# Four chained graph layers: in the relation stage every second gathered tile is turned by a transposing DMA instead of by TensorE

## The chip, the cores and the metric

The kernel runs on one core of one Trainium2 chip. The metric is device time in microseconds: the median of several executions, from which one execution was also recorded by the hardware profiler.

## The reference, cut to what matters

A feature matrix `x` of 1250 nodes by 768 goes through four graph layers (attention, GCN, attention with 12 heads, relational GCN), each followed by a residual sum and a layer norm. 20000 edges with one of 34 types each are given. The change lies in the fourth layer:

```python
seg  = edge_type * n + dst
agg  = segment_sum(x[src], seg, 34 * n)
mean = agg.reshape(34, n, -1) / maximum(cnt, 1).reshape(34, n, 1)
h1   = einsum('rni,rio->no', mean, W_rel) + x @ W_root + b_rgcn   # W_rel: 34 x 768 x 768
```

## The kernel before, in words

The fourth layer computes a message for each edge, not for each mean. Edges are sorted by relation and cut into RT = 190 tiles of P = 128 edges that hold one relation each, some 5.6 tiles to a relation. For a tile, 128 rows of `x3` are gathered, multiplied by that relation's 768 x 768 matrix, scaled by 1/count, and stored in `msg_d`; a later stage sums the messages by destination.

Numbers are float32, and the product is made in three parts, each operand being split into a rounded high part and the rest: high by high, high by low, low by high. A tile's product is 36 matmuls of 128 x 128 by 384: two halves of the output, three parts, KC = 6 blocks of 128 features. TensorE wants features on the partitions, so gathered rows (edges on partitions) are turned first, six 128 x 128 blocks to a tile.

The relation stage runs on all five sequencers, each in its own program order, tied by counting semaphores:

- **POOL** (`pool_rel`): gathers tile k+4 (L1885) into one of four row buffers `rows7` once tile k is turned, then subtracts for the low part of tile k (`low`, L1890).
- **PE** (`pe_rel`): turns tile k+2 into PSUM banks 0 to 3 (`turn`, L1912), then multiplies tile k into banks 4 to 7 (`messages`, L1924), two tiles deep.
- **ACT** (`act_rel`): `store` scales the product of tile k out of PSUM (L1961) and issues its DMA to `msg_d` (L1964); then `take` copies the turned tile k+3 twice out of PSUM, in full (L1953) and rounded (L1955), and raises `s_take7` (L1956), for which POOL's `low` and PE's next turn wait.
- **SP** (`sp_rel`): loads the next relation's matrix (L1853) as soon as the plain copy is split.
- **DVE** (`dve_rel`): splits that matrix into high and low (L1860, L1861) into the half of `wsplit` that the last but one relation has left.

Ahead of it the root stage handles the ten node tiles of `x3`: DVE sums and normalizes a tile (`rows`, with ACT's square root, L414, in the middle), POOL stores it to `x3_d` (L1821), PE turns it (L324) and multiplies it by `W_root` (L306), ACT copies the turned tile (L341), DVE adds the bias (L1792). The first gather waits for all ten stores.

Of the kernel before, what the change touches and what calls it, by code (L numbers as in the profile page):

```python
# [19 lines left out]
P = 128  # L20
# [3 lines left out]
D = 768  # L24
# [51 lines left out]
def build(nc, a, out):  # L76
    ctx = ExitStack()
    with ctx:
# [15 lines left out]
        x3_d = dram("x3_d", (NP, D))  # L94
        msg_d = dram("msg_d", (RT * P, D))
# [1678 lines left out]
        s_ready6, s_bias6 = sem("x3_ready"), sem("root_bias_in")  # L1774
        brow6 = work[:, 3 * KC * D:3 * KC * D + D]

        def dve_root(v, step):


            def rows(j):  # L1780
                z = z6[:, j, :]
                v.wait_ge(s_parts6[j % 2], 32 * (j // 2 + 1))
                step(v.tensor_tensor(z, z, parts6[0][:, j % 2, :], ALU.add))
                step(v.scalar_tensor_tensor(z, z, 0.0, parts6[1][:, j % 2, :], ALU.max, ALU.add))
                norm6.vector(v, step, z, j)
                v.sem_inc(s_ready6, 1)

            def product(j):
                if j == 0:
                    v.wait_ge(s_bias6, 16)  # L1790
                v.wait_ge(W_ROOT.product, W_ROOT.b["product"] + j + 3)
                v.tensor_tensor(halves(hbuf[:, j * D:(j + 1) * D]), W_ROOT.psum(j % 2), halves(brow6), ALU.add).then_inc(W_ROOT.emptied, 1)  # L1792
                if j == 7:
                    v.wait_ge(s_wrel, 16)
                    for u in range(2):
                        v.wait_ge(s_st6[u], 16 * (NT // 2))
                if j >= 7:
                    for c in (2 * (j - 7), 2 * (j - 7) + 1):
                        split7(v, step, 0, c)

            step.wait()
            for j in range(NT):
                rows(j)
                if j >= 2:
                    product(j - 2)
            for j in range(NT - 2, NT):
                product(j)

        def act_root(act):
            for j in range(2):  # L1810
                norm6.scalar(act, j)
            for j in range(NT):
                W_ROOT.take(act, j // 2, j % 2)
                if j + 2 < NT:
                    norm6.scalar(act, j + 2)

        def pool_root(g, step):
# [4 lines left out]
            for u in range(2):  # L1822
                g.wait_ge(s_st6[u], 16 * (NT // 2))

# [3 lines left out]
        rows7 = c7(GW * D).rearrange("p (u r n) -> p u r n", u=GW, r=1)  # L1828
        xt7 = c7(2 * D).rearrange("p (u c n) -> p u c n", u=2, c=KC)
        msg7 = c7(2 * D).rearrange("p (u n) -> p u n", u=2)  # L1830
        rows8 = c7(BT, I32)
# [5 lines left out]
        s_gath = [sem(f"rows_gathered{u}") for u in range(GW)]  # L1837
        s_turn7, s_take7, s_prod7, s_emp7, s_lo7 = (sem(n) for n in ("turned7", "taken7", "product7", "emptied7", "low_parts7"))
        s_split7 = sem("weights_split7")

        def sp_rel(sp):
# [6 lines left out]
            sp.dma_start(w, rel[0]).then_inc(s_wrel, 16)  # L1848
            for j in range(2, NT):
                sp_parts(sp, j)  # L1850
            with sp.Fori(0, R - 1) as i:
# [51 lines left out]
        def pe_rel(pe):  # L1903
# [3 lines left out]
            def turn(u, gathers, k):  # L1907
                pe.wait_ge(s_gath[u % GW], 16 * gathers)
                if not isinstance(k, int) or k >= 2:
                    pe.wait_ge(s_take7, k - 1)  # L1910
                for c in range(KC):
                    last = pe.transpose(ps[:, 2 * (u % 2) + c // 3, (c % 3) * P:(c % 3 + 1) * P], rows7[:, u % GW, 0, c * P:(c + 1) * P], ident[:, :])  # L1912
# [16 lines left out]
            for k in range(2):  # L1929
                turn(k, 1, k)  # L1930
            pe.wait_ge(W_ROOT.emptied, W_ROOT.b["emptied"] + NT + 2)
            whole = (RT - 2) // GW
            with pe.Fori(0, whole) as i:
                for u in range(GW):

                    turn(u + 2, i + 1 + (u + 2) // GW, GW * i + u + 2)
                    messages(GW * i + u, u)
            for k in range(whole * GW, RT):
                if k + 2 < RT:
                    turn(k + 2, (k + 2) // GW + 1, k + 2)  # L1940
                messages(k, k % GW)

        def act_rel(act, step):
# [3 lines left out]
            def take(k, u):  # L1947
                act.wait_ge(s_turn7, k + 1)
# [4 lines left out]
                step.count(act.activation(xt7[:, u % 2].rearrange("p (a b) n -> p a (b n)", a=2),  # L1953
                                          ps[:, 2 * (u % 2):2 * (u % 2) + 2, 0:HALF], ACT.Copy))
                step(act.activation(halves(xhi7[:, u % XW, :]), ps[:, 2 * (u % 2):2 * (u % 2) + 2, 0:HALF], ACT.Copy))  # L1955
                act.sem_inc(s_take7, 1)  # L1956

            def store(k, u, stores):
                act.wait_ge(s_prod7, k + 3)
                act.wait_ge(s_msgst[u % 2], 16 * stores)  # L1960
# [6 lines left out]
            for u in range(2):  # L1967
                act.sem_inc(s_msgst[u], 16)
            for k in range(2):
                take(k, k)  # L1970
            take(2, 2)
            for k in range(2):
                store(k, k, 1)
                take(k + 3, k + 3)
            whole = (RT - 5) // XW
            with step.loop(whole, 3 * XW) as i:
                for u in range(XW):
                    k = XW * i + u + 2
                    store(k, u + 2, 2 * i + 1 + (u + 2) // 2)
                    take(k + 3, u + 5)  # L1980
            for k in range(whole * XW + 2, RT):
                store(k, k, k // 2 + 1)
                if k + 3 < RT:
                    take(k + 3, k + 3)
            for u in range(2):
                act.wait_ge(s_msgst[u], 16 * (RT // 2 + 1))
# [219 lines left out]
```

## Time and profile before

| | |
|---|---|
| median of 3 runs | 3857.95 us (3854.33 to 3860.22) |
| the profiled execution | 3849.39 us, its span 3847.8 us |
| mean granted TensorE clock | 0.972 |
| PE busy | 3577.7 us, 93% of the span |
| ACT, DVE, POOL busy | 1667.7, 1926.0 and 1762.4 us |
| DMA | 468.18 MB, 122 GB/s on average |

The span runs from the first to the last instruction. Busy times are sums over an engine's instructions. The relation stage lies between 2065.8 us (its first turn) and 3386.2 us (its last store) of the span.

### The profile page before, as it was taken

To read this page: it belongs to the slowest core of one execution; us is meant where nothing else is said; L and a number is where in the kernel's file an instruction comes from. 1 tells how busy PE (TensorE), PEld (TensorE's weight loads), DVE (VectorE), ACT (ScalarE), POOL (GpSimd) and SP (SyncE) were. 2 spreads that over 40 slices of the span, in tenths; PEclk is the share of its full clock that TensorE was granted. 3 is DMA by queue.
4 is the path that set the end of the run, shared out by engine and by line. 5 is a ranking of instruction groups with operands and counts; after the bars stand their busy time and mean duration, and the time that the engine had idled before them with its cause. 6 is when DMAs were issued, how large, how long until landed. Compare 5 with 4: busy or idle time off the path is not lost.

```text
span 3847.8 us, 56876 instructions
## 1 busy us (share of the span) xinstructions
PE 3577.7 (93%) x18232; PEld 2940.5 (76%) x18233; DVE 1926.0 (50%) x2740; ACT 1667.7 (43%) x2919; POOL 1762.4 (46%) x1329
## 2 busy tenths in 40 slices
PE   8999779999798996799989999999999999989998
PEld 4654359999798995233347999999999999955598
DVE  8427788887335446999855233322333231023334
ACT  1117878888433212799942333333333333300021
POOL 6888888756100001776003444444444444357600
PEclk9999979999899998899989999999999999999999
DMA  3321123332423113211034555455555553379901
GB/s 109 104 61 23 35 55 86 90 87 63 132 80 121 45 62 103 74 42 42 28 119 153 188 188 186 166 188 187 186 175 173 187 188 114 102 267 305 271 17 69
DMA packets 176799, 468.18 MB, mean 122 GB/s; under 512 B 46100, under 2 KB 62539, under 8 KB 176677
## 3 DMA queue, kind: packets, MB, share of 16 engines
q0 software_dynamic: 59584, 185.70, 16.1%
q1 hardware_dynamic: 83972, 190.43, 15.0%
q10 hardware_dynamic: 33120, 90.52, 6.7%
q8 instruction: 64, 1.05, 0.1%
q14 instruction: 59, 0.48, 0.0%
HBM read 346.22 MB, written 119.79 MB: 121 GB/s over the span
## 4 chain that ended last, share of the span: by engine, by line
PE 41%; ACT 7%; POOL 5%; issue 3%; DVE 2%; DMA 1%; SPq 0%; POOLq 0%; DVEq 0%; ACTq 0%
PE ps L1924 31%; POOL work L2005 5%; ACT work L1304 4%; PE ps L1912 3%; ACT ps L1295 3%; PE ps L1587 3%; PE ps L306 2%; PE ps L298 2%; DVE work L1126 1%; PE ps L1241 1%; DVE work L1154 0%; ACT work L1314 0%; DMA ct<-x_d 0%; DMA work<-msg_d,ct 0%; PE ps L324 0%
## 5 line engine op out<-in xcount | busy, mean ns | idle before, releaser
L1924 PE MATMUL ps<-wsplit,xsplit 128*128 x6840 | 1237.2, 337 | 2.7 <-DVEq L1863 2.7
L1924 PEld LDWEIGHTS ps<-wsplit,xsplit 128*128 128x128 f32 x6840 | 1181.7, 188 | 3.0 <-issue 2.9
L1890 POOL TENSOR_TENSOR xsplit<-ct,xsplit 128x768 fp32r<-128x768 f32 x190 | 369.6, 1945 | 297.4 <-ACTq L1956 297.3
L1860 DVE CAST wsplit<-wplain 128x768 fp32r<-128x768 f32 x204 | 117.2, 574 | 759.8 <-PE ps L1924 743.0
L1304 ACT ACTIVATE work<-ps,work 128x418 f32<-128x418 f32 x720 | 438.4, 632 | 108.5 <-PE ps L1214 102.8
L1961 ACT ACTIVATE ct<-ps,invs 128x768 f32<-128x768 f32 x190 | 171.5, 903 | 710.8 <-PE ps L1924 710.8
L1251 PE MATMUL ps<-hbuf,work 128*128 128x193 f32 x2400 | 455.5, 328 | 15.2 <-DVE work L1168 13.1
L1251 PEld LDWEIGHTS ps<-hbuf,work 128*128 128x128 f32 x2400 | 408.4, 190 | 42.5 <-issue 16.8
L1295 ACT ACTIVATE ps<-work,lr 128x418 f32<-128x418 f32 x720 | 431.6, 634 | 6.1 <-DMA work<-lrow_d 6.1
L1154 DVE SCALAR_TENSOR_TENSOR work<-work,cnt 128x1250 f32<-128x1250 f32 x240 | 349.5, 1456 | 133.9 <-ACT work L1304 131.5
L1885 POOL DMA_INDIRECT ct<-x_d,relrec x190 | 200.9, 1057 | 454.8 <-PE ps L1912 443.2
L1241 PE MATMUL ps<-work,hbuf 128*65 128x512 f32 x720 | 324.6, 533 | 36.6 <-DVE work L1154 34.8
L298 PE MATMUL ps<-wsplit,xsplit 128*128 128x384 f32 x1800 | 337.3, 346 | 12.7 <-DVE xsplit L369 11.5
L298 PEld LDWEIGHTS ps<-wsplit,xsplit 128*128 128x128 f32 x1800 | 322.9, 195 | 14.9 <-issue 12.5
L800 POOL DMA_INDIRECT row_d<-hbuf x160 | 255.7, 1598 | 50.8 <-issue 48.5
L800 POOL DMA_INDIRECT relrec_d<-work x160 | 253.0, 1581 | 48.8 <-issue 48.8
L1214 PE MATMUL ps<-work 128*128 128x418 bf16 x720 | 247.6, 345 | 28.6 <-DMA work<-shift_d 24.3
L1348 POOL DMA_INDIRECT invs<-inv_d,relrec x190 | 220.0, 1158 | 118.1 <-issue 61.4
L2019 PE MATMUL ps<-work 128*128 128x384 f32 x784 | 256.8, 489 | 12.2 <-DMA work<-msg_d,ct 12.1
L1861 DVE TENSOR_TENSOR wsplit<-wplain,wsplit 128x768 fp32r<-128x768 f32 x204 | 246.0, 1206 | 7.1
L800 POOL DMA_INDIRECT dstrec_d<-work x160 | 215.9, 1349 | 66.3 <-issue 48.5
L2019 PEld LDWEIGHTS ps<-work 128*128 128x128 f32 x784 | 148.9, 191 | 119.8 <-issue 14.3
(217 smaller groups left out, 4254.1 us busy)
## 6 DMA issues: line engine op xcount, KB each, us to landing
wplain<-in_L_gnn_W_rel SPq DMA_DIRECT2D x34, 2304.0 KB, 9.5
msg_d<-ct ACTq DMA_DIRECT2D x190, 384.0 KB, 2.6
work<-lrow_d SPq DMA_DIRECT2D x47, 625.0 KB, 3.9
feat_d<-work ACTq DMA_DIRECT2D x30, 386.0 KB, 2.6
hbuf<-feat_d SPq DMA_DIRECT2D x60, 193.0 KB, 2.5
gat_d<-work POOLq DMA_DIRECT2D x12, 960.0 KB, 5.4
xplain<-gat_d SPq DMA_DIRECT2D x30, 384.0 KB, 3.1
wplain<-x_d SPq DMA_DIRECT2D x20, 384.0 KB, 3.1
```

What stands on the lines that cost most here:

```text
L298: last = pe.matmul(ps[:, 4 + 2 * u + h, 0:HALF], x[:, u, c * P:(c + 1) * P], w[:, c * D + h * HALF:c * D + (h + 1) * HALF], start=(q == 0 ...
L800: g.indirect_dma_start(out=(dstrec_d, relrec_d, row_d)[which], out_offset=bass.IndirectOffsetOnAxis((addr[:, 1, t:t + 1], addr[:, 0, t:t + ...
L1154: v.scalar_tensor_tensor(p[:, 0:N], p[:, 0:N], 1.0, cnt3[:, q % NT, 0:N], ALU.min, ALU.mult).then_inc(self.s_p, 1)
L1214: pe.matmul(ps[:, b, 0:c1 - c0], self.ones128, self.crow[h % 2][:, c0:c1], start=False, stop=True, skip_group_check=True).then_inc(self.s_ ...
L1241: last = pe.matmul(ps[0:C + 1, 3 + k, 0:n1 - n0], self.feat(h, s), p[:, n0:n1], start=(s == 0), stop=(s == NT - 1))
L1251: last = pe.matmul(ps[:, self.b0 + b, t * (C + 1):(t + 1) * (C + 1)], p[:, dt * P:(dt + 1) * P], self.feat(h, s), start=(s == 0 and t == 0 ...
L1295: act.activation(ps[:, b, 0:c1 - c0], self.Rb[h % 2][:, c0:c1], ACT.Relu, bias=lr[:, col:col + 1]).then_inc(self.s_relu, 1)
L1304: act.activation(self.p[q % 3][:, c0:c1], ps[:, b, 0:c1 - c0], ACT.Exp, bias=self.l2[:, col:col + 1], scale=1.0 - SLOPE)\
L1861: step(v.tensor_tensor(wlo7[:, at:at + D], w, whi7[:, at:at + D].bitcast(F32), ALU.subtract))
L1890: g.tensor_tensor(xlo7[:, k % XW, :], xt7[:, k % 2].rearrange("p c n -> p (c n)"), xhi7[:, k % XW, :].bitcast(F32), ALU.subtract).then_inc ...
L1924: last = pe.matmul(ps[:, 4 + 2 * (u % 2) + h, 0:HALF], x[:, u, c * P:(c + 1) * P], w[:, bass.ds(base + (c * D + h * HALF), HALF)], start=( ...
L2019: last = pe.matmul(ps[:, 2 * (u % 2) + h, 0:HALF], sel8[:, GT * (u % 2) + w, :], mg8[:, GT * u + w, h * HALF:(h + 1) * HALF], start=(w == ...
```

## The change

The tiles of even number go on as before: they are gathered as float32 rows into `rows7`, now one buffer, and PE turns them. The tiles of odd number are not turned by PE. A transposing DMA moves 2-byte elements, so `x3` is stored a second time with each row's 768 low half-words ahead of its 768 high half-words (`x3p_d`). An odd tile gathers rows of this copy into one of two buffers (`halfs7`), ACT issues one SBUF-to-SBUF transposing DMA of 128 x 1536 half-words into `plane7`, and ACT's `take` puts the half-words together: one copy of 1536 elements with interleaved output in place of the full copy from PSUM, then the rounded copy from SBUF. The buffers fill the room of the four former row buffers.

In the root stage ACT makes each tile's planes ahead of its `take`, SP stores them, the split of the first matrix waits for the planes of all tiles, and the first gather for their stores. `plane6` is the room of `msg7`, and its stores count on the semaphores of the message stores.

```diff
 # act_root, sp_rel, pool_root, dve_root
             for j in range(NT):
+                act.wait_ge(s_ready6, j + 1)
+                if j >= 2:
+                    act.wait_ge(s_msgst[j % 2], 16 * (j // 2))
+                act.activation(plane6[:, j % 2, :].rearrange("p (t n) -> p t n", t=2),
+                               z6[:, j, :].bitcast(U16).rearrange("p (n t) -> p t n", t=2), ACT.Copy).then_inc(s_plane6, 1)
                 W_ROOT.take(act, j // 2, j % 2)
...
+            def planes(j):
+                sp.wait_ge(s_plane6, j + 1)
+                sp.dma_start(x3p_d[j * P:(j + 1) * P, :], plane6[:, j % 2, :]).then_inc(s_msgst[j % 2], 16)
             for j in range(2, NT):
                 sp_parts(sp, j)
+                planes(j - 2)
...
                 g.wait_ge(s_st6[u], 16 * (NT // 2))
+                g.wait_ge(s_msgst[u], PLANES)
...
                     v.wait_ge(s_wrel, 16)
+                    v.wait_ge(s_plane6, NT)
 # pool_rel
             def gather(k):
-                if k >= GW:
-                    g.wait_ge(s_turn7, k - GW + 1)
-                g.indirect_dma_start(out=rows7[:, k % GW, 0, :], out_offset=None, in_=x3_d,
+                if k % 2 == 0 and k >= 2:
+                    g.wait_ge(s_turn7, k // 2)
+                if k % 2 == 1 and k >= 5:
+                    g.wait_ge(s_cross7, 16 * ((k - 4) // 2 + 1))
+                g.indirect_dma_start(out=rows7 if k % 2 == 0 else halfs7[:, k // 2 % 2, :], out_offset=None,
+                                     in_=x3_d if k % 2 == 0 else x3p_d,
...
-            for k in range(GW):
+            for k in (1, 0, 3):
                 gather(k)
             for k in range(RT):
-                if k + GW < RT:
-                    gather(k + GW)
+                ahead = k + (2 if k % 2 == 0 else 4)
+                if ahead < RT:
+                    gather(ahead)
                 low(k)
 # pe_rel
+                for u in range(2, XW + 2):
+                    k = XW * i + u
+                    if u % 2 == 0:
+                        turn(u + 2, i + 1 + (u + 2) // XW, k + 2)
+                    messages(k, u % XW)
 # act_rel
+            def cross(u, gathers, taken=True):
+                act.wait_ge(s_gath[u % GW], 16 * gathers)
+                if taken:
+                    act.sem_inc(s_take7, 1)
+                act.dma_start_transpose(plane7.rearrange("p (c r) -> p c r", r=P), halfs7[:, u // 2 % 2, :]).then_inc(s_cross7, 16)
...
+                if u % 2 == 0:
+                    pair = ps[:, 2 * (u // 2 % 2):2 * (u // 2 % 2) + 2, 0:HALF]
+                    step.count(act.activation(halves(x), pair, ACT.Copy))
+                    step(act.activation(halves(xhi7[:, u % XW, :]), pair, ACT.Copy))
+                else:
+                    step(act.activation(x.bitcast(U16).rearrange("p (n t) -> p t n", t=2), plane7.rearrange("p (t n) -> p t n", t=2), ACT.Copy))
+                    step(act.activation(xhi7[:, u % XW, :], x, ACT.Copy))
+                    act.sem_inc(s_take7, 1)
...
             with step.loop(whole, 3 * XW) as i:
                 for u in range(XW):
                     k = XW * i + u + 2
                     store(k, u + 2, 2 * i + 1 + (u + 2) // 2)
-                    take(k + 3, u + 5)
+                    take(k + 3, u + 5, 2 * i + (u + 5) // 2 + 1)
+                    if u % 2 == 1:
+                        cross(u + 6, i + (u + 6) // XW + 1)
```

Before the loop ACT issues the transfer of tile 1, takes tiles 0, 1 and 2, issues that of tile 3, and goes on in the loop's order.

## Rows read from the trace of the kernel before

**Rows 1.** Page, engines: busy us (share of the span) and instructions.
```profile
PE 3577.7 (93%) x18232; PEld 2940.5 (76%) x18233; DVE 1926.0 (50%) x2740; ACT 1667.7 (43%) x2919; POOL 1762.4 (46%) x1329
```

**Rows 2.** Busy time by stretch: engines' busy us, granted clock, DMA share, GB/s.
```profile
2200.00:2600.00 400.00, 400.00 (x2431) 398.00 (x2430) 124.58 (x140) 139.91 (x174) 174.71 (x116) 1.00 0.53 179
2600.00:3000.00 400.00, 400.00 (x2429) 398.01 (x2428) 120.00 (x136) 139.42 (x174) 175.68 (x116) 1.00 0.54 185
```

**Rows 3.** Waits by pair, 2100 to 3386 us: us in total, times, longest.
```profile
DVE wsplit L1860 <- PE ps L1924: 743.0, 32, 23.6
ACT ct L1961 <- PE ps L1924: 689.2, 186, 5.3
POOL ct L1885 <- PE ps L1912: 423.1, 178, 2.8
```

**Rows 4.** Timeline, ACT's stores of tiles 0, 186, 187, 188 and 189.
```profile
2080.30 0.90 ACT L1961 ACTIVATE ct<-ps,invs 128x768 f32<-128x768 f32 x1 [8.24 <-PE ps L1924]
...
3366.80 0.90 ACT L1961 ACTIVATE ct<-ps,invs 128x768 f32<-128x768 f32 x1 [3.63 <-PE ps L1924]
...
3373.71 0.90 ACT L1961 ACTIVATE ct<-ps,invs 128x768 f32<-128x768 f32 x1 [3.89 <-PE ps L1924]
...
3379.95 0.91 ACT L1961 ACTIVATE ct<-ps,invs 128x768 f32<-128x768 f32 x1 [5.34 <-PE ps L1924]
...
3386.19 0.90 ACT L1961 ACTIVATE ct<-ps,invs 128x768 f32<-128x768 f32 x1 [5.34 <-PE ps L1924]
```

**Rows 5.** Timeline of one tile in mid-stage.
```profile
2605.77 0.82 PE L1912 MATMUL ps<-ident,ct 128*128 128x128 f32 x6
2606.15 0.90 ACT L1961 ACTIVATE ct<-ps,invs 128x768 f32<-128x768 f32 x1 [3.80 <-PE ps L1924]
...
2606.34 6.50 PE L1924 MATMUL ps<-wsplit,xsplit 128*128 x36
2606.86 0.96 POOL L1885 DMA_INDIRECT ct<-x_d,relrec  x1 [2.01 <-PE ps L1912]
2607.30 0.34 ACTq L1964 DMA_DIRECT2D msg_d<-ct  x1
2607.84 0.81 ACT L1953 ACTIVATE ct<-ps 128x768 f32<-128x768 f32 x1 [0.79 <-ACT ct L1961]
2608.55 0.81 ACT L1955 ACTIVATE xsplit<-ps 128x768 fp32r<-128x768 f32 x1
2609.48 1.85 POOL L1890 TENSOR_TENSOR xsplit<-ct,xsplit 128x768 fp32r<-128x768 f32 x1 [1.66 <-ACTq L1956]
```

**Rows 6.** DMA issues by line: count, KB each, median us to landing.
```profile
wplain<-in_L_gnn_W_rel SPq DMA_DIRECT2D x34, 2304.0 KB, 9.5
msg_d<-ct ACTq DMA_DIRECT2D x190, 384.0 KB, 2.6
...
ct<-x_d,relrec POOLq DMA_INDIRECT x190, 4.6
...
shift_d<-work SPq DMA_DIRECT2D x96, 1.9 KB, 1.4
```

**Rows 7.** L1964's own view: its DMA's landing times.
```profile
DMA to landing us min/median/max: 2.3/2.6/7.7
```

**Rows 8.** DMA queue of the scatters, 200 to 400 us: packets, MB, share of 16 engines.
```profile
q0 software_dynamic: 3824, 0.71, 8.2%
```

**Rows 9.** Timeline of the root stage: its start, one tile, its end.
```profile
1986.90 0.20 ACT L414 ACTIVATE small<-small 128x1 f32<-128x1 f32 x1 [13.77 <-DVE small L407]
1987.01 0.79 ACT L341 ACTIVATE ct<-ps 128x768 f32<-128x768 f32 x1
...
1989.46 10.25 PE L306 MATMUL ps<-mask,ct 128*128 128x384 f32 x24
...
2012.60 0.20 ACT L414 ACTIVATE small<-small 128x1 f32<-128x1 f32 x1 [7.50 <-DVE small L407]
2012.71 0.79 ACT L341 ACTIVATE ct<-ps 128x768 f32<-128x768 f32 x1
...
2017.00 7.91 PE L306 MATMUL ps<-mask,ct 128*128 128x384 f32 x24
...
2046.19 0.20 ACT L414 ACTIVATE small<-small 128x1 f32<-128x1 f32 x1 [7.50 <-DVE small L407]
...
2051.01 0.55 DVE L1860 CAST wsplit<-wplain 128x768 fp32r<-128x768 f32 x1
2051.30 1.14 POOL L1885 DMA_INDIRECT ct<-x_d,relrec  x1 [2.81 <-DMA x_d<-work]
...
2066.08 1.47 PE L1912 MATMUL ps<-ident,ct 128*128 128x128 f32 x12
...
2067.17 0.97 POOL L1885 DMA_INDIRECT ct<-x_d,relrec  x1 [10.06 <-PE ps L1912]
...
2072.11 8.15 PE L1924 MATMUL ps<-wsplit,xsplit 128*128 x36 [2.70 <-DVEq L1863]
```

More of the change, by code:

```diff
@@ L1848, in sp_rel @@
             sp.dma_start(w, rel[0]).then_inc(s_wrel, 16)
+            def planes(j):
+                sp.wait_ge(s_plane6, j + 1)
+                sp.dma_start(x3p_d[j * P:(j + 1) * P, :], plane6[:, j % 2, :]).then_inc(s_msgst[j % 2], 16)
             for j in range(2, NT):
                 sp_parts(sp, j)
+                planes(j - 2)
+            for j in range(NT - 2, NT):
+                planes(j)
             with sp.Fori(0, R - 1) as i:
@@ L1908, in turn @@
                 pe.wait_ge(s_gath[u % GW], 16 * gathers)
-                if not isinstance(k, int) or k >= 2:
-                    pe.wait_ge(s_take7, k - 1)
+                if not isinstance(k, int) or k >= 4:
+                    pe.wait_ge(s_take7, k - 3)
                 for c in range(KC):
-                    last = pe.transpose(ps[:, 2 * (u % 2) + c // 3, (c % 3) * P:(c % 3 + 1) * P], rows7[:, u % GW, 0, c * P:(c + 1) * P], ident[:, :])
+                    last = pe.transpose(ps[:, 2 * (u // 2 % 2) + c // 3, (c % 3) * P:(c % 3 + 1) * P], rows7[:, c * P:(c + 1) * P], ident[:, :])
                 last.then_inc(s_turn7, 1)
@@ L1927, in messages @@
                 last.then_inc(s_prod7, 1)
-            for k in range(2):
-                turn(k, 1, k)
+            turn(0, 1, 0)
             pe.wait_ge(W_ROOT.emptied, W_ROOT.b["emptied"] + NT + 2)
-            whole = (RT - 2) // GW
+            turn(2, 1, 2)
+            messages(0, 0)
+            messages(1, 1)
+            whole = (RT - 4) // XW
             with pe.Fori(0, whole) as i:
[L1934 to L1941, printed above, removed]
+                for u in range(2, XW + 2):
[3 more added lines that the diff above has]
+                    messages(k, u % XW)
+            for k in range(whole * XW + 2, RT):
+                if k % 2 == 0 and k + 2 < RT:
+                    turn(k + 2, (k + 2) // XW + 1, k + 2)
+                messages(k, k % XW)
         def act_rel(act, step):
@@ L1966, in act_rel @@
             act.sem_inc(s_emp7, 2)
[L1967 to L1975, printed above, removed]
+            cross(1, 1, taken=False)
+            take(0, 0, 1)
+            act.sem_inc(s_take7, 1)
+            take(1, 1, 1)
+            take(2, 2, 2)
+            cross(3, 1)
+            store(0, 0, 1)
+            take(3, 3, 2)
+            store(1, 1, 1)
+            take(4, 4, 3)
+            cross(5, 2)
+            whole = (RT - 6) // XW
             with step.loop(whole, 3 * XW) as i:
@@ L1983, in act_rel @@
                 if k + 3 < RT:
-                    take(k + 3, k + 3)
+                    take(k + 3, k + 3, (k + 3) // 2 + 1)
+                    if k % 2 == 1:
+                        cross(k + 4, (k + 4) // XW + 1)
             for u in range(2):
-                act.wait_ge(s_msgst[u], 16 * (RT // 2 + 1))
+                act.wait_ge(s_msgst[u], PLANES - 16 + 16 * (RT // 2 + 1))
         UP = 4
```

24 lines of the change are left out of this document (15 added, 9 removed).

## The prediction, made before the changed kernel ran

> **What bounds the kernel now.** I read the page's engine line first: PE is busy for 93% of the span [rows 1]. That is a mean over stages, so I cut the relation stage into stretches: there PE is busy for every one of 400 us, at a granted clock of 1.00 (the 2.4 GHz level), while ACT is busy for 140 us, POOL for 175 and the DMA engines for 0.53 to 0.54 of the time [rows 2]. The waits say the same from the other side: ACT, DVE and POOL all wait for PE, ACT 689 us in 186 waits [rows 3], and PE waits for nobody. So what leaves PE's queue comes off the time, as long as ACT, which gets the work, still ends first.
>
> The price of a turn is seen best in ACT's stores, which follow the products. From tile 0 to tile 187 they are (3373.71 - 2080.30) / 187 = 6.917 us apart, and each of these steps holds one turn. The last two tiles have no turn ahead of them, since all tiles are turned by then: 6.24 us each [rows 4]. A turn thus costs PE 0.677 us, a little more than the 0.57 us between its first transpose and the first product matmul [rows 5].
>
> **What the change takes from PE.** Of the 187 steps, the 94 with an odd tile lose their turn: 94 x 0.677 = 63.6 us. Nothing is added to PE's queue. A pair of tiles goes from 13.83 to 2 x 6.24 + 0.677 = 13.16 us.
>
> **What it gives to ACT.** Before, a tile costs ACT 3.21 us, from the start of its store (2606.15) to the end of the rounded copy (2608.55 + 0.81), the issue of the message's DMA (0.34 us) included; then it idles 3.6 to 3.9 us until the next product ends [rows 4, 5]. In a pair after the change it does, in this order: store and even take, 3.21 us; the wait for the odd tile's gather and the issue of its transposing transfer, c; store of the next tile, 0.90 + 0.79 = 1.69 us; the wait for the transfer's landing, L after its issue began; the odd take. That take is two copies one after the other. By the rows, 1 element costs 0.20 us and 768 cost 0.81 [rows 5, 9], which is 0.8 ns an element, so 1536 elements cost 0.20 + 1.23 = 1.43 us; no row has 2-byte elements interleaved, so I bound it by 0.81 and by twice as much, 2.9, and take 1.43. With the second copy (0.81) and 0.16 of gaps, 2.4 us. ACT's shortest pair is 3.21 + max(L, c + 1.69) + 2.4 us. It stays under PE's 13.16 as long as L is at most 7.55 us and c at most 5.86.
>
> **L and c** are what the trace does not show. From below: 384 KB from the same queue, the message store, land in 2.6 us [rows 6]. From above: a block row of 128 half-words is 256 B, so a tile is 128 x 12 = 1536 pieces. The scatters, the rows with small packets, take 0.082 x 16 x 200 / 3824 = 69 ns a packet [rows 8]; 1536 x 69 / 16 = 6.6 us, and with the landing of a tiny transfer, 1.4 us [rows 6], L = 8.0 us. The gather (the same bytes into SBUF, 4.6 us, rows 6) is the nearest row; the finer pieces put L above it. I take 5.3 us, the middle. Higher still lies a transfer that turns its twelve 128 x 128 blocks one after another: 12 x 1.4 = 16.8 us; that is a rival below. c is bounded by one DMA issue of 0.34 us and twelve of them, 4.1 [rows 5]; both are inside 5.86, so c costs nothing in the steady state. With L = 5.3 ACT's pair is 10.9 us, 2.2 us short of PE's, and hidden.
>
> Two rules of the Trainium skill disagree about L. "DMA: Bandwidth & Descriptors", section "Latency and other measured facts", gives a transposing DMA 261 GB/s in one kernel: by it, as an estimate, 393 KB take 1.5 us and L is near 2.9, well hidden. "VectorE: DVE Perf Modes", section "The three transpose paths", gives the DMA 1309 ns for one 128 x 128 block of 2-byte elements, against 390 for TensorE: twelve times that is 15.7 us, an estimate, and the change would lose heavily. No row of this trace has such a transfer.
>
> **Waits added, and who stands behind them.** Behind the wait for the gather on ACT stand the rise of `s_take7` for the even tile and the next store. That gather is issued once the same buffer's transfer two pairs earlier has landed, some 26 us ahead of its use less L, against 4.6 us of landing: hidden. The even tiles now have one row buffer: POOL gathers the next when PE has turned the last, and the next turn comes 13.16 us later; issue 0.96 and landing 4.6 us leave 7.6 us. POOL's low part of an even tile (1.85 us) is released by ACT some 3.3 us after the tile's turn and is wanted two tiles after it: hidden. Odd `take` plus low part end about 13 us after the release of ACT's pair, and the tile's product starts 20 us after it: 7 us in hand.
>
> **Root stage.** Each tile gains a plane copy, 1.43 us, and a 384 KB store. PE sets the pace there, its 24 matmuls filling 7.91 us of 8.4; ACT idles 7.50 us a tile [rows 9]. In mid-stage the copy moves the end of the turned tile's copy from 2013.5 to 2014.9, and the matmuls that want it begin at 2017.0. At the start it moves 1987.8 to 1989.2, the matmuls beginning at 1989.46; at 2.9 us it would cost 1.2 us once. At the end: from 2046.4 two plane copies and one take (3.65 us) put the last plane at 2050.0, and DVE's split, which now waits for it, starts at 2051.01. SP issues the plane stores between loads that are a tile early. The first gather moves from 2051.3 to between 2052.7 and 2058 (landing as in [rows 7]), and its rows are wanted at 2066. I cost all that at 0.
>
> **Start of the relation stage.** The gather of tile 2 now waits for the turn of tile 0: as the one at 2067.17, it lands 4.6 us later, at 2071.8, and its turn stands ahead of the first product: 2072.45 against 2072.11 [rows 9]. Before its first take ACT issues a transfer; take and low part (3.4 us) after 2066.9 + c hold the product up once c is over 1.8 us, by 2.3 us at c = 4.1. I take 1 us for both.
>
> **Sum** on the profiled execution: 3849.4 - 63.6 + 1 = 3786.8 us. That execution lies 8.6 us under the median of the runs (3857.95), and on the median's footing it is **3795 us**, 1.6% less.
>
> **Rivals.**
> 1. Hidden only in part: the packet price, L = 8.0. ACT's pair is 13.6 us, the gain 0.22 x 95 - 1 = 20 us: 3838. For it: pieces are small and 0.54 of the DMA engines' time is taken; against it: the packets of the scatters go to scattered rows in DRAM. From L of about 8.1 to 8.3 on, no change: 3850 to 3866.
> 2. Slower: ACT becomes the bound. Place: the wait of the odd take for the transfer. Point: L over 8.2 us (7.55 + 0.677). Price: 95 us for each us of L beyond it; L = 10 gives (10 - 7.55) x 95 - 62.6 = +170, **4028 us**. For it: message stores land in 2.6 us at the median but in 7.7 at worst [rows 7]; were the transfer tripled so in one pair of each relation, as the matrix of 2304 KB loads (33 loads of 9.5 us), those pairs would run 8.4 us over, of which the second PSUM buffer covers some 5.3, and 33 x 3.1 = 102 us are lost: 3897. Against it: the bytes, which are those of a message.
> 3. The blocks go one after another, L = 16.8: ACT's pair is 22.4 us, +9.25 x 95 - 62.6 = +816: 4674.
> 4. The change does not do what it says: a turn's 0.677 us is partly a break between products that stays. Then the 0.57 us of the transposes alone come off: 3805, inside the forecast's own range.
>
> **Chances.** Forecast with rival 4, 0.54 (3785 to 3810); rival 1, 0.09, and no change, 0.06; rival 2, 0.23; rival 3, 0.08. The measurement of this kernel tells about 0.2% (7.7 us) from nothing. Faster 0.63, same 0.06, slower 0.31. The range of 8 in 10 goes from 3783 to 4030: it leaves out rival 3, the worst third of rival 2 and a little below. The likeliest case alone: 3785 to 3810.
>
> **What would show it.** Right: 570 transposes in the relation stage instead of 1140; stores 6.24 and 6.92 us apart in turn; ACT's stores still released by PE; transfers landing within 7.5 us; root tiles still 8.4 us apart. Rivals 1 to 3: ACT's first odd copy released by the transfer at the end of a long wait, PE idle ahead of products until ACT's store or POOL's low part. The forecast is wrong if L is over 7.55 us, or if PE idles in the stage for another reason.

## The result, and the profile after

The changed kernel took 3790.84 us at the median (3786.62 to 3796.04 in 4 executions), beside 3857.95 us before: ratio 0.9832, 95% interval 0.9818 to 0.9846. The forecast was 3795 us, that is 63 us less; the medians lie 67 us apart. The execution that was profiled took 3791.21 us, its span 3789.6.

The page's engine line answers to [rows 1]: 585 fewer matmuls are recorded (the transposes, counted by their weight loads, go from 1140 to 570, as forecast; not every matmul is recorded). ACT is busy for 137 us more, and PE keeps its 93%.

```profile
PE 3509.1 (93%) x17647; PEld 2879.3 (76%) x17663; DVE 1956.8 (52%) x2740; ACT 1804.7 (48%) x2929; POOL 1751.0 (46%) x1329
```

The two stretches of [rows 2] again (busy us of PE, PEld, DVE, ACT and POOL, then granted clock, DMA share, GB/s), and under them the whole relation stage, from the start of the first store to the start of the last:

```profile
2200.00:2600.00 400.00, 400.00 (x2372) 398.97 (x2372) 139.39 (x144) 186.26 (x182) 178.24 (x122) 1.00 0.72 220
2600.00:3000.00 400.00, 400.00 (x2375) 398.93 (x2374) 141.70 (x147) 186.91 (x184) 180.29 (x122) 1.00 0.72 220
...
2083.51:3325.80 1242.29, 1242.26 (x7362) 1238.74 (x7360) 386.15 (x406) 575.67 (x563) 546.53 (x371) 1.00 0.70 209
```

The same view of the kernel before, for the stage that [rows 4] delimits:

```profile
2080.30:3386.19 1305.89, 1305.85 (x7926) 1299.13 (x7924) 356.15 (x406) 454.07 (x563) 557.65 (x370) 1.00 0.50 170
```

PE is busy all through in both. It has 7926 - 7362 = 564 = 94 x 6 transposes less, and the stage is 1305.89 - 1242.29 = **63.6 us** shorter, the predicted term. ACT's busy time went up by 122 us and the DMA share from 0.50 to 0.70, and neither shows in the end.

The waits of 2100 to 3325 us (total, times, longest) answer to [rows 3]. PE still has no line of its own there. ACT's wait for the product fell from 689.2 to 457.0 us; new are 61.9 us of its wait for the transfer, and POOL's wait for it ahead of a gather, which the second half-word buffer covers:

```profile
DVE wsplit L1880 <- PE ps L1948: 659.2, 32, 21.9
ACT ct L2004 <- PE ps L1948: 457.0, 168, 5.3
POOL ct L1907 <- DMA ct<-ct: 275.6, 89, 6.6
ACT ct L1997 <- DMA ct<-ct: 61.9, 38, 2.9
```

One pair of tiles in the timeline (start, duration, engine, line; in brackets the idle time before it and what ended it) answers to [rows 5]:

```profile
2596.83 0.91 ACT L2004 ACTIVATE ct<-ps,invs 128x768 f32<-128x768 f32 x1 [3.82 <-PE ps L1948]
...
2598.60 1.96 ACT L1997 ACTIVATE ct<-ct 128x1536 uint16<-128x1536 uint16 x1 [0.86 <-ACT ct L2004]
2600.59 0.85 ACT L1998 ACTIVATE xsplit<-ct 128x768 fp32r<-128x768 f32 x1
2602.67 0.82 PE L1936 MATMUL ps<-ident,ct 128*128 128x128 f32 x6
2602.97 0.90 ACT L2004 ACTIVATE ct<-ps,invs 128x768 f32<-128x768 f32 x1 [1.53 <-PE ps L1948]
2603.24 12.74 PE L1948 MATMUL ps<-wsplit,xsplit 128*128 x72
...
2606.37 1.83 ACTq L1980 DMA_TRANSPOSE ct<-ct  x1
2609.95 0.90 ACT L2004 ACTIVATE ct<-ps,invs 128x768 f32<-128x768 f32 x1 [3.76 <-PE ps L1948]
```

PE turns once and then runs 72 matmuls of two products without a break. ACT's stores are 6.14 and 6.98 us apart, 13.12 for the pair (predicted 13.16), and each is still released by PE after an idle wait. The half-words are put together by the copy of 1.96 us, which here waits for ACT's own store alone: the transfer had landed by then.

The transfer in its line's own view (durations in ns, min/median/max, first and last start; then landing):

```profile
L1980 ACTq DMA_TRANSPOSE ct<-ct x95: 1375/2025/5490, 2067.7 to 3303.6; - x95
...
DMA to landing us min/median/max: 3.7/4.3/10.8
```

So L is 4.3 us where 5.3 was taken, and issuing holds ACT's queue 2.0 us, near the middle of the bounds 0.34 and 4.1. Two of the 95 transfers, beside loads, landed later than the 7.55 us that the prediction allows (8.2 and 10.8); PE idled for neither.

Between the two profiled executions lie 58.2 us, not 63.6. Three of the missing us are ahead of the first store, which comes at 2083.51 instead of 2080.30. Of these, 1.3 were there when the root stage ended and are not the change's: the layer ahead, which it leaves alone, ended 2.5 us later in this execution, and the root stage itself took 1.2 us less. The other 1.9 are the change's, against the 1 taken. From the first turn to the first product pass 7.41 us instead of 6.03, PE waiting for tile 2's gather as foreseen, and the first product, behind this longer wait, takes 0.5 us more:

```profile
2067.39 0.82 PE L1936 MATMUL ps<-ident,ct 128*128 128x128 f32 x6
...
2073.50 1.51 PE L1936 MATMUL ps<-ident,ct 128*128 128x128 f32 x6 [5.29 <-DMA ct<-x_d,relrec]
2074.80 14.92 PE L1948 MATMUL ps<-wsplit,xsplit 128*128 x72
```

Behind the last store 2.2 us more pass (463.8 against 461.6), in stages that the change leaves alone.

### The profile page after: what moved, and what is told of

The parts are those of the page before. It is cut to its first block, busy times and chain, and to the rows that moved or that the text cites. A ratio compares the mean times of both kernels' runs of the same rounds, so it can differ in the third digit from the quotient of the medians.

```text
span 3789.6 us, 56202 instructions
## 1 busy us (share of the span) xinstructions
PE 3509.1 (93%) x17647; PEld 2879.3 (76%) x17663; DVE 1956.8 (52%) x2740; ACT 1804.7 (48%) x2929; POOL 1751.0 (46%) x1329
## 3 DMA queue, kind: packets, MB, share of 16 engines
q10 hardware_dynamic: 182080, 127.88, 12.0%
## 4 chain that ended last, share of the span: by engine, by line
PE 40%; ACT 7%; POOL 5%; issue 3%; DVE 2%; DMA 1%; SPq 0%; POOLq 0%; DVEq 0%; ACTq 0%
PE ps L1948 31%; POOL work L2055 5%; ACT work L1305 4%; ACT ps L1296 3%; PE ps L1588 3%; PE ps L307 2%; PE ps L1936 2%; PE ps L299 2%; DVE work L1127 1%; PE ps L1242 1%; DVE work L1155 0%; ACT work L1315 0%; DMA ct<-x_d 0%; DMA work<-msg_d,ct 0%; PE ps L325 0%
## 5 line engine op out<-in xcount | busy, mean ns | idle before, releaser
L1948 PE MATMUL ps<-wsplit,xsplit 128*128 x6840 | 1212.8, 336 | 0.0
L1913 POOL TENSOR_TENSOR xsplit<-ct,xsplit 128x768 fp32r<-128x768 f32 x190 | 361.4, 1902 | 368.6 <-ACTq L1999 240.8
L1880 DVE CAST wsplit<-wplain 128x768 fp32r<-128x768 f32 x204 | 137.7, 675 | 680.1 <-PE ps L1948 659.2
L299 PE MATMUL ps<-wsplit,xsplit 128*128 128x384 f32 x1800 | 336.7, 345 | 12.7 <-DVE xsplit L370 11.9
L2069 PE MATMUL ps<-work 128*128 128x384 f32 x784 | 257.2, 490 | 12.7 <-DMA work<-msg_d,ct 12.6
L1881 DVE TENSOR_TENSOR wsplit<-wplain,wsplit 128x768 fp32r<-128x768 f32 x204 | 253.8, 1244 | 7.1
L1997 ACT ACTIVATE ct<-ct 128x1536 uint16<-128x1536 uint16 x95 | 186.1, 1959 | 111.8 <-DMA ct<-ct 65.8
## 6 DMA issues: line engine op xcount, KB each, us to landing
wplain<-in_L_gnn_W_rel SPq DMA_DIRECT2D x34, 2304.0 KB, 10.5
```

Source lines behind the costliest of these rows:

```text
L299: last = pe.matmul(ps[:, 4 + 2 * u + h, 0:HALF], x[:, u, c * P:(c + 1) * P], w[:, c * D + h * HALF:c * D + (h + 1) * HALF], start=(q == 0 ...
L1881: step(v.tensor_tensor(wlo7[:, at:at + D], w, whi7[:, at:at + D].bitcast(F32), ALU.subtract))
L1913: g.tensor_tensor(xlo7[:, k % XW, :], xt7[:, k % 2].rearrange("p c n -> p (c n)"), xhi7[:, k % XW, :].bitcast(F32), ALU.subtract).then_inc ...
L1948: last = pe.matmul(ps[:, 4 + 2 * (u % 2) + h, 0:HALF], x[:, u, c * P:(c + 1) * P], w[:, bass.ds(base + (c * D + h * HALF), HALF)], start=( ...
L2069: last = pe.matmul(ps[:, 2 * (u % 2) + h, 0:HALF], sel8[:, GT * (u % 2) + w, :], mg8[:, GT * u + w, h * HALF:(h + 1) * HALF], start=(w == ...
```

## The experiments

All are made from the changed kernel except the last. The stage is from the start of the first store to that of the last in the profiled execution; PE idle is the stage less PE's busy time in it. Ratios are to the kernel before as it ran beside each experiment, where its median was 3852.49 to 3856.71 us.

| kernel | median us | ratio, 95% | stage us | PE idle us | clock |
|---|---|---|---|---|---|
| before | 3857.95 | 1 | 1305.89 | 0.0 | 1.00 |
| changed | 3790.84 | 0.9832 (0.9818 to 0.9846) | 1242.29 | 0.0 | 1.00 |
| e1, no transfers | 3794.02 | 0.9836 (0.9813 to 0.9860) | 1242.29 | 0.0 | 1.00 |
| e5, half transfers | 3791.33 | one execution | 1242.29 | 0.0 | 1.00 |
| e2, odd turns given back | 3908.28 | 1.0128 (1.0100 to 1.0156) | 1371.29 | 45.1 | 0.99 |
| e9, as e2, loads 3 us later | 3859.59 | 1.0000 (0.9988 to 1.0012) | 1305.55 | 0.8 | 1.00 |
| e8, loads 6 us later | 3804.52 | 0.9849 (0.9826 to 0.9872) | 1265.53 | 16.4 | 0.99 |
| e3, one copy more | 3885.86 | 1.0074 (1.0049 to 1.0099) | 1335.56 | 60.0 | 0.98 |
| e4, two copies more | 4019.96 | 1.0422 (1.0397 to 1.0447) | 1473.34 | 161.1 | 0.97 |
| e7, three of four tiles | 3868.78 | 1.0041 (1.0023 to 1.0060) | 1312.06 | 76.8 | 0.98 |
| e10, as e7, POOL stores | 3903.31 | 1.0125 (1.0108 to 1.0141) | 1341.06 | 95.6 | 0.97 |
| e11, all tiles, POOL stores | 3971.04 | 1.0310 (1.0288 to 1.0331) | 1406.47 | 154.4 | 0.94 |
| e6, before with one block | 3800.84 | one execution | 1253.88 | 0.0 | 1.00 |

### e1_no_transfer: what do the transfers cost?

```diff
 def cross(u, gathers, taken=True):
     act.wait_ge(s_gath[u % GW], 16 * gathers)
     if taken:
         act.sem_inc(s_take7, 1)
+    if taken:
+        act.sem_inc(s_cross7, 16)
+        return
     act.dma_start_transpose(...)
```

> The changed kernel, but 94 of its 95 transposing transfers are left out: ACT raises their semaphore itself, and every odd tile takes the planes of the first transfer (so the odd messages are not the reference's). Gathers, plane copies and takes stay. Theory (PE sets the pace, the transfers are wholly hidden): the same time as the changed kernel, 3791 us within 0.2%, stores 13.14 us apart by pairs. Rival (the transfers, which raise the DMA engines' share from 0.54 to 0.72, hold up gathers, matrix loads or ACT): faster than the changed kernel by what they cost, 10 us or more. Either way the landing of the matrix loads should fall back from 10.5 to about 9.5 us.

The stage is the same to the hundredth of a us, 1242.29, with the DMA share at 0.51 in place of 0.70. The 94 transfers therefore cost no time in the changed kernel, and what is gained is PE's turns alone. One expectation missed: the matrices, whose landing rose from 9.5 us [rows 6] to 10.5, still take 10.4 without the transfers, so these aren't what slows them.

### e2_turns_back: give PE the odd turns again, the transfers staying

```diff
+def idle_turn(k, u):
+    pe.wait_ge(s_take7, k)
+    for c in range(KC):
+        pe.transpose(ps[:, 2 * ((u + 3) // 2 % 2) + c // 3, ...], ident[:, :], ident[:, :])
 ...
     if u % 2 == 0:
         turn(u + 2, i + 1 + (u + 2) // XW, k + 2)
+    else:
+        idle_turn(k, u)
     messages(k, u % XW)
```

> The changed kernel with six more transposes on PE ahead of each odd tile of the loop (of a constant, into a PSUM pair that is free; nobody reads them). Transfers and takes stay. Theory (the whole gain is the 94 turns that left PE's queue): 92 turns of 0.677 us come back, +62 us, 3853, the time of the kernel before within 0.2%; stores 13.8 us apart by pairs. Rival (part of the gain comes from elsewhere, such as ACT or the gathers): clearly less than +62, 20 to 45 us.

The turns' price was expected and almost twice as much came: +117 us at the median, +129.0 in the stage of the profiled execution. The stage by windows, and its waits of PE:

```profile
2092.69:3463.98 1371.29, 1326.22 (x7914) 1315.25 (x7912) 383.80 (x406) 575.27 (x564) 553.35 (x371) 0.99 0.70 189
```

```profile
PE ps L1953 <- POOL xsplit L1913: 43.9, 15, 3.8
```

PE idles 45.1 us, nearly all in 15 gaps of some 3 us ahead of a product, and is busy for 1326.2 us where the kernel before needs 1305.85 for as many matmuls: 20.4 us more. So 63.6 for the turns, 45.1 idle and 20.4 of slower matmuls make up the 129. The timeline shows one gap:

```profile
2563.02 2.16 ACTq L1987 DMA_TRANSPOSE ct<-ct  x1
2563.85 0.37 SPq L1873 DMA_DIRECT2D wplain<-in_L_gnn_W_rel  x1
...
2579.70 1.93 ACT L2004 ACTIVATE ct<-ct 128x1536 uint16<-128x1536 uint16 x1 [12.14 <-DMA ct<-ct]
2579.80 0.96 POOL L1907 DMA_INDIRECT ct<-x3p_d,relrec  x1 [14.47 <-DMA ct<-ct]
2582.63 1.80 POOL L1913 TENSOR_TENSOR xsplit<-ct,xsplit 128x768 fp32r<-128x768 f32 x1 [1.88 <-ACTq L2006]
2584.64 3.71 PE L1953 MATMUL ps<-wsplit,xsplit 128*128 x14 [3.74 <-POOL xsplit L1913]
```

0.83 us after the transfer began to be issued, SP issued the load of the next matrix. The transfer, 4.5 us at the median, landed just ahead of 2579.70, over 16 us after its start. ACT waited 12.14 us for it, POOL's low part came late, and PE stood. All 15 gaps follow such a transfer, each with a load issued 0.46 to 1.10 us after its start, and these transfers landed after 12.5 to 16.6 us.

The load suffers as well. It landed after 19.7 us. Its line's own view has 12.4 us at the median and 19.8 at most, where the median in the changed kernel is 10.5:

```profile
DMA to landing us min/median/max: 9.7/12.4/19.8
```

The DMA queues show what happens (packets, MB, share of the 16 engines; q10 carries ACT's transfers, q1 SP's loads). In the changed kernel, around its load at 2319.98, the packets of a transfer run from 2318 to 2321 us with none of the load among them, and the load's follow, here from 2321 to 2331:

```profile
q10 hardware_dynamic: 1568, 0.39, 76.1%
...
q1 hardware_dynamic: 784, 2.36, 67.1%
```

In e2, from 2566 to 2576 us, the packets of both run side by side:

```profile
q10 hardware_dynamic: 981, 0.30, 59.8%
q1 hardware_dynamic: 411, 1.25, 55.7%
```

A packet of the transfer then takes 0.598 x 16 x 10 us / 981 = 98 ns instead of 0.761 x 16 x 3 us / 1568 = 23, and one of the load 217 ns instead of 137. So the load doesn't push the transfer behind it, as the expectations of e9 and e8 have it (overtaking): the two mix, and both slow down.

How fast PE goes around the gap:

```profile
2570.00:2580.00 10.00, 10.00 (x62) 9.96 (x61) 0.00 (x0) 0.30 (x1) 0.20 (x1) 1.00 0.93 204
2580.00:2584.60 4.60, 0.90 (x8) 0.62 (x6) 0.00 (x0) 3.43 (x4) 2.57 (x3) 1.00 0.49 170
2584.60:2588.00 3.40, 3.36 (x14) 3.37 (x15) 0.00 (x0) 1.46 (x2) 2.67 (x2) 0.71 0.73 232
2588.00:2592.00 4.00, 4.00 (x21) 4.00 (x20) 0.00 (x0) 2.25 (x2) 1.05 (x2) 0.82 0.79 196
2592.00:2600.00 8.00, 8.00 (x52) 7.93 (x51) 7.05 (x6) 3.97 (x6) 5.39 (x3) 1.00 0.52 156
```

After the idle 3.74 us the granted clock is 0.71 and then 0.82, parts of these stretches at the 1.2 GHz level, and the product takes 8.11 us instead of 6.50. A gap of 3.7 us thus cost 5.3, and fifteen such tails of up to 1.6 us are the size of the 20.4 us.

In the changed kernel the loads fall elsewhere. Half of them come 3.0 us after a transfer's start, when its issue has just ended, and such a transfer lands after 4.2 to 4.7 us:

```profile
2316.92 2.08 ACTq L1980 DMA_TRANSPOSE ct<-ct  x1
...
2319.98 0.37 SPq L1873 DMA_DIRECT2D wplain<-in_L_gnn_W_rel  x1
...
2321.53 0.96 POOL L1907 DMA_INDIRECT ct<-x3p_d,relrec  x1 [2.59 <-DMA ct<-ct]
```

(POOL's gather is released by the landing.) Nearly all others come 4.8 to 5.1 us ahead of a transfer, which then lands within 7.2 us but for the two named above. One load, early in the stage, does come 0.89 us after a transfer's start (2120.31). That transfer's packets had nearly all gone when the load's began, and it landed after 6.5 us without a wait of PE. So my theory after e2 was the phase between load and transfer, and its rival that PE's added work makes the stall. e9 and e8 change the phase and DVE's work alone.

### e9_turns_back_load_later and e8_load_later: move the load instead

```diff
-    step(v.tensor_tensor(wlo7[:, at:at + D], w, ..., ALU.subtract))
+    for _ in range(1 + again * (c == KC - 1)):
+        step(v.tensor_tensor(wlo7[:, at:at + D], w, ..., ALU.subtract))
     if c == KC - 1:
         v.sem_inc(s_split7, 1)        # SP's next load waits for it
```

with `again` 3 beside e2's idle turns (e9), and 6 without them (e8).

> The kernel with PE's idle turns, its loads issued 3 us later by three more steps on DVE. Theory (overtaking): loads at +0.8 move to +3.8, behind the issue, and those at -4.5 to -1.5; the transfers of 15 us and more go away or get fewer, the loss of PE with them, and what is left over the changed kernel is the 62 us of the turns and at most 25 more: 3855 to 3880 instead of 3908. Rival: as before the shift, 3908.

PE's work is e2's; only DVE's last split step is repeated, so that SP issues each load some 3 us later. After the first few relations the loads come, in turn, some 6 us after a transfer's start and 0.95 to 1.6 us ahead of one. In the second case the load's packets go first, and the transfer lands after 9.2 to 10.3 us. The stage:

```profile
2098.72:3404.27 1305.55, 1304.75 (x7914) 1297.57 (x7912) 515.91 (x505) 575.54 (x564) 565.57 (x371) 1.00 0.66 199
```

PE's idle time went from 45.1 to 0.8 us (all of it behind the one transfer whose load came at its very start, and which landed after 13.6 us) and the clock back to 1.00; the stage is within 0.4 us of the stage before the change, the ratio 1.0000, and the median, 3859.59 us, lies where it was expected. The odd turns cost 63.3 us and the phase of the load all the rest.

> The changed kernel with the last step of each relation's split done six times more on DVE, which has some 20 us of waiting a relation: the next matrix load is issued 5.9 us later, nothing else moves. In the changed kernel loads come 3.0 us after the issue of a transfer has begun (its 2.2 us of issue are over, it lands after 4.6 us) or 4.9 us before it (it lands after 7.1 us); in the kernel with PE's idle turns half of them come 0.8 us after, inside the issue, and those transfers land after 15 to 16.7 us. Theory (a load that is issued while a transfer is still being issued overtakes it, and the transfer lands behind it): loads at -4.9 move to about +1.0, their transfers land after 14 us or more, and about 2.8 us of PE are lost for each of them, some 16: +30 to +60 us on the changed kernel's 3791. Rival (PE's idle turns themselves, or the traffic as such, cost those 48 us): no change.

The other direction was to bring the fault into the changed kernel. It did so only in part: 4 transfers were caught, with loads 0.4 to 0.9 us after their start, and landed after 12.4 to 17.1 us; a fifth, with a load 0.6 us ahead, landed after 11.4. PE waited 16.3 us in 5 gaps, one behind each, the longest 5.6. Half of the loads were late enough to release DVE's splits themselves (225 us in 17 waits), and so drifted to other phases. At the median 3804.52 us, +14 where 30 to 60 were expected, with intervals that overlap. The count of the transfers caught was missed. The price of one caught, 16.3 / 5 = 3.3 us of idle time, is near that of e2, 43.9 / 15 = 2.9. As PE has no idle turns here, they aren't what makes the stall.

### e3_one_copy and e4_two_copies: how much room has ACT?

```diff
-    step(act.activation(x.bitcast(U16)..., plane7..., ACT.Copy))
+    for _ in range(2):                 # e4: 3
+        step(act.activation(x.bitcast(U16)..., plane7..., ACT.Copy))
```

> The changed kernel with the copy that interleaves the planes done twice in each odd take: 1.96 us and a gap more on ACT per pair, after the landing of the transfer. Theory (ACT runs a chain in which the landing counts whole: 3.24 + 0.2 + 4.3 + 2.98 = 10.7 us of the pair's 13.14, 2.4 us in hand): 12.7 us, no change, 3791 within 0.2%. Rival A (all of ACT's idle time, 519 us over 93 pairs, 5.6 us each, is in hand): no change either. Rival B (the hand is already empty because the landing stretches beside the matrix loads, up to 10.8 us): +20 to +100 us.

> The same copy done three times, 4.0 us more on ACT per pair. Theory (chain with the landing in it, 2.4 us in hand, 95 us for each us beyond): 14.7 us a pair, +1.6 x 94 = +150 us, about 3941, and stores of even tiles no longer released by PE. Rival A (5.6 us in hand): no change, 3791. Rival B (nothing in hand): +300 us or more.

Both were to tell whether all of ACT's idle time is in hand, or only what its chain with the landing leaves. The e4 timeline of ACT has one pair that no load disturbs:

```profile
3302.20 0.90 ACT L2005 ACTIVATE ct<-ps,invs 128x768 f32<-128x768 f32 x1 [0.33 <-ACT xsplit L1999]
...
3305.60 2.11 ACTq L1980 DMA_TRANSPOSE ct<-ct  x1
3308.28 0.90 ACT L2005 ACTIVATE ct<-ps,invs 128x768 f32<-128x768 f32 x1 [2.85 <-issue]
...
3310.06 5.97 ACT L1998 ACTIVATE ct<-ct 128x1536 uint16<-128x1536 uint16 x3 [0.88 <-DMA ct<-ct]
3316.06 0.85 ACT L1999 ACTIVATE xsplit<-ct 128x768 fp32r<-128x768 f32 x1
3317.25 0.90 ACT L2005 ACTIVATE ct<-ps,invs 128x768 f32<-128x768 f32 x1 [0.34 <-ACT xsplit L1999]
```

The stores no longer wait for PE: ACT goes round in 3317.25 - 3302.20 = 15.05 us, of which 0.88 us is waiting for the landing. Less the two extra copies (5.97 - 1.96 = 4.0) it is 11.05, so the changed kernel has 13.14 - 11.05 = **2.1 us** in hand a pair, not the 5.6 of its waits for PE and for the transfer ((457.0 + 61.9) / 93). The prediction had 2.2. With one copy more (e3) the undisturbed pair is 13.05, still inside; yet e3 lost 95 us, where this theory had said 0: its rival, that the pairs beside a load are not made up again, was right (20 to 100 expected). Beside a load L rises to as much as 9.6 us, twice to 10.9 and 12.7, and the pair to as much as 17; behind the last load PE is busy throughout. PE idled for 60.0 us of the stage, and the other 33 of its 93.3 us are slower matmuls, at a mean clock of 0.98. e4 lost 229 us, where +150 was expected and the chain of the undisturbed pair gives 95 x 1.9 = 180; pairs beside a load, 16 to 18 us long, make up the rest. In its stage, 231.1 us longer, PE idles for 161.1 us and is busy for 70.0 us more, at a clock of 0.97.

### e7, e10 and e11: turn more tiles by transfer

```diff
-    if u % 2 == 0:
+    if u == 2:                         # e11: no turn at all
         turn(u + 2, i + 1 + (u + 2) // XW, k + 2)
 ...
-    act.dma_start(msg_d[...], msg7[...])   # e10 and e11: POOL issues it, ahead of its gather
```

> The changed kernel with three of four tiles turned by transfer (those with k mod 4 not 0) instead of two; same buffers. PE loses 47 more turns: -32 us if all stays hidden. Theory (ACT's chain counts the landing, since there is one plane buffer): a transfer tile after a transfer tile takes 4.5 + 2.95 + 0.1 = 7.55 us, a group of four 3 x 7.55 + 3.4 = 26.0 us against PE's 25.64, so ACT sets the pace, and the transfers that lie beside a load (some 33 to 50, 2.6 us and more each) are no longer made up for: 3830 to 3890 us. Rival A (ACT's work alone counts, 22.7 us a group): 3759. Rival B (overtaken transfers of 15 us in most relations): over 3900.

> The kernel with three of four tiles by transfer, and POOL instead of ACT issues the DMAs of the messages (and of the plane stores of the root stage), which takes 0.8 us a tile off ACT. Theory (ACT sets the pace of the kernel with three of four): a transfer tile after another takes ACT 3.8 to 4.5 + 2.95 + 0.1 = 6.9 to 7.5 us and the even tile 2.6, 23 to 25 us a group against PE's 25.64; the steady state is PE's again, what the loads stretch is made up for in part: 3765 to 3830 us instead of 3869. Rival (POOL's queue becomes the bound, or the DMA engines, at 0.74 of the time): no better than 3869.

> All tiles by transfer, no turn on PE in the stage (-64 us against the changed kernel if all is hidden: 3727), POOL issues the stores as in the kernel before this one, and the room of the float rows becomes a second plane buffer, so that a transfer is issued a tile ahead and its landing leaves ACT's chain. ACT per tile: 0.9 + 0.1 + 1.5 to 2.2 of issue + 2.95 + 0.2 = 5.7 to 6.35 us against PE's 6.24. Theory (the landing counted because of the one buffer): about PE's pace, less what issues stretched by loads (up to 5 us) cost, 34 x 1 to 3 us: 3740 to 3830. Rival (DMA engines full: 0.74 of the time with three of four, all of it here): over 3870.

All three lose (e11 also has a second plane buffer, which the diff above leaves out). e7 came inside its 3830 to 3890 us. It spares PE another 47 turns, 31.8 us, and loses 76.8 to idling and 24.8 to slower matmuls. Its stretches while matrices load and after the last one, and its largest wait of PE in 2100 to 3400 us:

```profile
2200.00:2600.00 400.00, 372.74 (x2100) 366.80 (x2100) 128.46 (x132) 190.17 (x169) 166.34 (x112) 0.97 0.74 219
...
3200.00:3390.00 190.00, 190.00 (x1112) 189.76 (x1111) 14.35 (x22) 99.61 (x89) 80.65 (x56) 1.00 0.60 164
```

```profile
PE ps L1948 <- ACTq L2006: 62.5, 35, 4.3
```

Beside the loads ACT's `store` and its signal, behind landings that ACT waits for in turn, release PE late. Behind the last load (issued at 3182.3) PE is busy for all of 190 us: with no load about, three of four tiles by transfer stay hidden, and the theory that ACT sets the pace throughout fell. For e10 and e11 I expected a gain from taking the message issues off ACT, to 3765 to 3830 and 3740 to 3830; both were slower than e7, as their rivals had it. In e10, too, PE is busy for all of the 150 us from 3250, behind the last load, but only for 365 to 375 of 400 beside loads. In e11 it idles for 9.5 of 170 us even behind the last load (3310 to 3480), and beside loads the DMA share is the highest of all:

```profile
2200.00:2600.00 400.00, 352.83 (x1898) 345.65 (x1897) 120.01 (x123) 196.37 (x159) 186.94 (x159) 0.94 0.81 220
```

There transfers land after 5.8 us, gathers after 5.7, messages after 4.5 and matrices after 12.7. Whether the DMA engines' load or POOL's order (store, gather, low part) sets its pace stays open; no run parts the two.

### e5_half_transfer and e6_before_one_block: two prices by themselves

```diff
 # e5, the changed kernel
-    act.dma_start_transpose(plane7..., halfs7[:, u // 2 % 2, :])
+    act.dma_start_transpose(plane7[:, 0:blocks]..., halfs7[:, u // 2 % 2, 0:blocks])   # blocks = D
 # e6, the kernel before
-    for c in range(KC):
+    for c in range(KC if u % 2 == 0 else 1):
         last = pe.transpose(...)
```

> The changed kernel, each transfer but the first with 6 of its 12 blocks of columns (the low half-words; the high ones stay those of the first, so odd messages are not the reference's). Theory (a fixed landing of about 2.4 us behind an issue that goes by blocks): the issue falls from 2.0 to about 1.0 us and the landing from 4.3 to about 3.3; time unchanged, 3791. Rival (a fixed price per transfer): both stay. Rival (all by blocks): landing 2.2.

```profile
L1981 ACTq DMA_TRANSPOSE ct<-ct x95: 1237/1242/1397, 2066.8 to 3301.7; - x95
...
DMA to landing us min/median/max: 2.8/3.4/9.2
```

Six blocks instead of twelve: landing 3.4 us for 4.3, issue 1.24 for 2.03. A block costs (4.3 - 3.4) / 6 = 0.15 us of landing behind some 2.5 us that don't depend on the size; of two sizes alone, this is an estimate. The least issue falls by less than the median, from 1.38 to 1.24 us, so that the issue doesn't simply go by blocks. The time is unchanged.

> The kernel before, where PE turns only the first of six blocks of each odd tile (so odd messages are not the reference's); no transfer, no planes. Theory (a turn's 0.677 us go by blocks): a step with an odd tile falls by 0.56 us, stores of a pair 13.83 - 0.56 = 13.27 us apart, -53 us. Rival (part of the 0.677 is a break between products that stays): -40 us or less.

ACT's stores in e6, one pair:

```profile
2604.81 0.90 ACT L1961 ACTIVATE ct<-ps,invs 128x768 f32<-128x768 f32 x1 [3.02 <-PE ps L1924]
2611.82 0.91 ACT L1961 ACTIVATE ct<-ps,invs 128x768 f32<-128x768 f32 x1 [3.81 <-PE ps L1924]
2618.08 0.90 ACT L1961 ACTIVATE ct<-ps,invs 128x768 f32<-128x768 f32 x1 [3.06 <-PE ps L1924]
```

The pair is 2618.08 - 2604.81 = 13.27 us: 13.83 less five transposes of 0.677 / 6 = 0.113 us. The stage is 52.0 us shorter than before, where 53 were expected. The price goes by the blocks, no part of it is a break that would stay, and the prediction's rival 4 falls.

## Why the prediction was right, point by point

- **What bounds it.** Right. PE is busy for all of the stage before and after, and e1 and e5 move DMA and ACT's queue without moving the end.
- **94 x 0.677 = 63.6 us.** Right to 0.1 us; e9, which gives the turns back, returns 63.3, and e6 shows the price by blocks.
- **ACT's pair.** The form 3.21 + max(L, c + 1.69) + odd take was right but for some gaps, the terms off in both directions. L was 4.3 (taken 5.3), c 2.0 (0.34 to 4.1), the odd take 1.96 + 0.85 + gaps = 2.95 us (taken 2.4). The interleaving copy, an estimate of 1.43 by elements, takes 1.96, inside the bounds 0.81 and 2.9; the copy in the root stage, whose output runs on in order, takes 1.47. With these terms the formula gives 10.5 us, and e4's chain 11.05, the rest being gaps between its parts that the form leaves out. That the prediction's 10.9 is so near is luck: an L taken 1 us too long makes up for a take and gaps taken too short.
- **The packet price, rival 1.** Mis-sized. The queue of the transfers answers to [rows 8]: `q10` went from 33120 to 182080 packets, 148960 / 95 = 1568 to a transfer, as the 1536 pieces suggest, and from 6.7% of 3847.8 us to 12.0% of 3789.6, times 16 engines: 197.0 x 16 / 148960 = 21 ns a packet, not the scatters' 69. L = 8.0 was out of reach by that. The middle of the two ends, the choice made, erred by 1 us.
- **Blocks in series, rival 3.** Fell: 0.15 us for each further block, not 1.4. The Trainium skill ("VectorE: DVE Perf Modes", section "The three transpose paths") gives the DMA 1309 ns for one block; twelve in one transfer don't cost twelve times that here. The 261 GB/s that the Trainium skill gives in "DMA: Bandwidth & Descriptors", section "Latency and other measured facts", are near the slope, 32 KB in 0.15 us or 218 GB/s, but leave out the 2.5 us that come first.
- **ACT becomes the bound, rival 2.** It did not happen in the changed kernel. Its special case, a transfer slowed in one pair of each relation as the matrix loads, was priced at 33 x 3.1 = 102 us. That is the right place and the right price for a relation hit: e2 loses 2.9 us of idle time in each of 15 relations, and up to 1.6 more to the lower clock, which the prediction didn't count. What the prediction lacked is the condition. It is not enough that the load is under way; its packets have to mix with the transfer's. In e2 and e8 that befell all 19 transfers with a load issued 0.4 to 1.1 us after their start. In the changed kernel only one load comes so close, and its transfer got by; half of the others come 3.0 us after a transfer's start, and by the records of single packets the load's first then starts 4.1 us after that start, just as the transfer's last one ends (3.7 to 4.2 us after it). That the forecast held is therefore in part luck: it rests on a phase that I had not worked out and that is nowhere written in the code.
- **Waits added, root stage, start.** Right within their size: root tiles stay 8.40 us apart, no wait of PE in the steady state comes from the added semaphores, and the start cost 1.9 us in place of 1. The root stage was costed at nothing, and so it was: from the last DVE step of the layer ahead to the last matmul of the root stage pass 107.9 us before and 106.7 after, and 107.8 in e5, which has the same root stage.

## What to carry to other kernels

Room on a helper engine is what its chain leaves, issues and landings included, not its idle time: ACT waited 5.6 us a pair for PE and the transfer and had 2.1 in hand. That was enough away from the loads; beside them one copy more, or one tile more in four by transfer, was already a loss. Before relying on a transfer that lands within a few us, lay its issue beside those of the large periodic loads on the other queues; if they can drift into each other, fix the distance in the code, since a shift of 3 us was worth 44 us of idle time and 20 of slower matmuls here. An operation moved off a saturated engine paid here, to 0.1 us in 63.6, its step in that engine's stream, read from the spacing of what follows it, and that spacing can be had from the trace before.

## What the runs showed of the hardware that was not expected

- A transposing transfer whose packets mix with those of a 2304 KB load on the other queue lands some 12 to 17 us after its start, in place of 4.3 (loads 0.4 to 1.1 us after that start, in e2 and e8), and most of these loads land after 17 to 20 us in place of 10.5. Issued 0.95 to 1.6 us behind the load (in e9) it lands after 9.2 to 10.3, some 5 us behind mostly within 7.2, and 3.0 us ahead as usual. Why packets of both kinds take longer side by side no run shows.
- The issue of a transposing transfer holds the issuing engine's queue: 1.24 us for six blocks (e5) and 2.03 for twelve at the median, up to 5.49; the issue of a plain message store of the same bytes takes 0.34 [rows 5].
- A copy of 1536 2-byte elements takes 1.96 us with interleaved output and 1.47 with contiguous output from interleaved input.
- A gap of 3.7 us on PE was followed by 7 us at a granted clock of 0.71 to 0.82, and by a product of 8.11 us instead of 6.50.
